# Sixteen blocks instead of thirteen fetched row by row by SyncE and ScalarE, in a gather and scatter kernel of a graph network

## The reference

```python
h = jnp.maximum(_layernorm(x, axis=-1), 0.0)
h0 = pe_val @ W0 + b0
t = gelu(h0) @ W1 + b1
t = gelu(t) @ W2 + b2
score = (h0 + t) @ W3 + b3
msg = h[src] * score
sums = segment_sum(msg, dst, num_segments=n)
cnt = segment_sum(ones, dst, num_segments=n)
out = x + (sums / jnp.maximum(cnt, 1.0)) @ Wo + bo
```

## Time and profile before

| | |
|---|---|
| median of 3 runs | 3926.53 us (3926.48 to 3933.37) |
| profiled execution, its time | 3928.06 us |
| profiled execution, its span | 3926.3 us |
| mean granted TensorE clock | 0.788 |
| PE busy | 3063.5 us, 78% |
| POOL busy | 2948.4 us, 75% |
| DVE busy | 1299.3 us, 33% |
| ACT busy | 850.0 us, 22% |
| row transfers on SPq | 7904 |
| row transfers on ACTq | 5408 |

### The profile page before, as it was taken

The page is one execution under the profiler, slowest core; times in us unless marked ns, Lnnn a source line. Parts: engine busy times, 40 slices in busy tenths (PEclk is TensorE's granted clock), DMA queues, the critical chain, the costliest instruction groups (busy, mean ns, idle before and its releaser), DMA issues.

```text
span 3926.3 us, 55941 instructions
## 1 busy us (share of the span) xinstructions
PE 3063.5 (78%) x8729; PEld 1466.1 (37%) x8730; DVE 1299.3 (33%) x2572; ACT 850.0 (22%) x1241; POOL 2948.4 (75%) x3125
## 2 busy tenths in 40 slices
PE   3886878777778778778877778788778777778778
PEld 1443333333333333333333333333333333333345
DVE  7333323333223333223333223333223333223334
ACT  4222212122222222222122212122222122222111
POOL 7777777777777777777777777777777777777775
PEclk9888778778777778778778777777777778778767
DMA  6122221111111111111111111111111111111112
GB/s 161 42 44 44 44 43 42 41 41 42 41 41 41 44 39 44 39 44 41 41 41 41 41 41 41 43 42 39 44 41 41 41 41 41 41 41 41 44 35 58
DMA packets 164649, 176.52 MB, mean 45 GB/s; under 512 B 86257, under 2 KB 86386, under 8 KB 163984
## 3 DMA queue, kind: packets, MB, share of 16 engines
q0 software_dynamic: 99808, 102.40, 13.7%
q1 hardware_dynamic: 53112, 67.00, 6.0%
q10 hardware_dynamic: 11432, 4.61, 0.4%
HBM read 167.34 MB, written 6.40 MB: 44 GB/s over the span
## 4 chain that ended last, share of the span: by engine, by line
POOL 61%; issue 21%; PE 11%; SPq 2%; DMA 2%; DVE 1%; ACTq 1%; ACT 0%; DVEq 0%; POOLq 0%
POOL rows L414 61%; DMA rows<-h_rows,idx 2%; SPq L367 2%; PE ps_wb L613 1%; PE ps_wa L613 1%; PE ps_h1a L593 1%; PE ps_h1a L590 1%; PE ps_h1b L583 1%; PE ps_h1b L593 1%; PE ps_sb L602 1%; ACTq L542 1%; PE ps_h1b L590 1%; PE ps_sa L602 1%; PE ps_h1a L583 1%; PE ps_h0b L574 1%
## 5 line engine op out<-in xcount | busy, mean ns | idle before, releaser
L414 POOL DMA_INDIRECT rows<-h_rows,idx x3071 | 2902.4, 945 | 937.0 <-issue 924.5
L613 PE MATMUL ps_wb<-ln_sq,msg 128*128 128x128 f32 x1608 | 324.0, 364 | 447.8 <-DVE acc L970 437.5
L844 DVE TENSOR_TENSOR msg<-ps_sb,rows 128x512 f32<-128x512 f32 x194 | 133.9, 690 | 1162.2 <-DMA rows<-h_rows,idx 1162.2
L844 DVE TENSOR_TENSOR msg<-ps_sa,rows 128x512 f32<-128x512 f32 x196 | 135.3, 691 | 1142.5 <-DMA rows<-h_rows,idx 1142.5
L613 PE MATMUL ps_wa<-ln_sq,msg 128*128 128x128 f32 x1616 | 289.5, 334 | 284.5 <-DVE acc L970 278.3
L613 PEld LDWEIGHTS ps_wb<-ln_sq,msg 128*128 128x128 f32 x1608 | 275.7, 259 | 611.3 <-DVE acc L970 563.7
L964 DVE TENSOR_REDUCE hot_sum<-ln_sq 128x64 f32<-128x512 f32 x403 | 415.1, 1030 | 13.3
L613 PEld LDWEIGHTS ps_wa<-ln_sq,msg 128*128 128x128 f32 x1616 | 245.1, 232 | 443.6 <-DVE acc L970 398.0
L486 ACT ACTIVATE score_t<-ps_h1a,b_last 128x512 f32<-128x512 f32 x202 | 138.9, 688 | 1094.5 <-PE ps_h1a L593 974.9
L486 ACT ACTIVATE score_t<-ps_h1b,b_last 128x512 f32<-128x512 f32 x201 | 138.2, 687 | 894.6 <-PE ps_h1b L593 767.8
L590 PE MATMUL ps_h1a<-attr,w_attr 64*128 64x512 f32 x404 | 319.3, 881 | 0.0
(11 more groups left out here) (102 smaller groups left out, 2096.4 us busy)
## 6 DMA issues: line engine op xcount, KB each, us to landing
ln_sq<-h_rows SPq DMA_DIRECT2D x7904, 0.2 KB
ln_sq<-h_rows ACTq DMA_DIRECT2D x5408, 0.2 KB
attr<-in_edges SPq DMA_DIRECT2D x201, 256.0 KB
rows<-h_rows,idx POOLq DMA_INDIRECT x3071, 2.6
xs<-in_x SPq DMA_DIRECT2D x4, 700.0 KB
h_rows<-ln_d ACTq DMA_DIRECT2D x4, 700.0 KB
dst_i<-in_dst SPq DMA_DIRECT2D x1, 1612.0 KB, 26.9
rows<-in_dst_rows SPq DMA_DIRECT2D x4, 384.0 KB
```

What stands on the lines that cost most here:

```text
L414: pool.indirect_dma_start(rows[:, slot, t, :], None, table, bass.IndirectOffsetOnAxis(ap=idx[:, s, t:t + 1], axis=0),).then_inc(gathered[s ...
L613: pe.matmul(window[0:m * D, 0:m * WIN], msg[:, s % 2, t:t + m, :].rearrange("p t d -> p (t d)"), hot[:, k, t:t + m, :].rearrange("p t n -> ...
L844: dve.tensor_tensor(msg[:, s % 2, 0:n, :], ps_s[s % 2][:, 0:n * D].rearrange("p (t d) -> p t d", d=D), near, ALU.mult).then_inc(msg_done, 1)
```

## The change

PERIOD goes from 31 to 25, so 16 blocks are fetched row by row: 23, 48, and so on to 398 (SPARE_AT = PERIOD - 2). SyncE brings 18 parts of each (576 rows) and ScalarE 14 (448 rows). SyncE's count of rows ahead of each attr load goes from 20 to 24 per block, ScalarE's from twice 7 to twice 9 per step. In all SyncE issues 9216 rows instead of 7904, ScalarE 7168 instead of 5408, and GpSimd 24 gathers fewer.

```diff
-PERIOD = 31
+PERIOD = 25
 SPARE_AT = PERIOD - 2
 SPARES = len(range(SPARE_AT, NB, PERIOD))
 SPARE_BUFS = 2
 LOADED = 32
...
-SP_PARTS = 19
-SP_ROWS = 20
-ACT_ROWS = 7
+SP_PARTS = 18
+SP_ROWS = 24
+ACT_ROWS = 9
```

## The result

| | before | changed |
|---|---|---|
| median | 3926.51 us (3925.52 to 3933.37, 4 runs) | 4022.89 us (4020.37 to 4029.74, 4 runs) |
| span of the profiled execution | 3926.3 us | 4020.3 us |
| mean granted TensorE clock | 0.788 | 0.791 |
| DVE line 844 waiting for gathered rows | 2304.7 us | not in the list |
| PE waiting for attr | 31.7 us | 788.2 us |

The changed kernel is 2.5% slower; 4013 us was forecast, with a range of 3978 to 4038 us.

The account below looks back on a forecast made before the run. SyncE's queue, with attr behind 24 rows per block (9.81 us), was to replace GpSimd as bound: last attr landed at 3843 us, plus 43, 57, 60 and 10 us of tail, gave 4013 us, range 3978 to 4038 us.

Parts of the forecast that it names:

- GpSimd's saving: On GpSimd's gather queue: three more blocks left out, 24 gathers at 1.250 us each, so the gathers end 30.0 us earlier.
- SyncE's pace: SyncE's queue: 24 row issues per block ahead of attr cost 9.81 us a block, against GpSimd's 9.6 us.
- the saturated stretch: Early part of SyncE's queue, attr issues from 163.0 to 544.4 us, giving 12.80 us per part of 32 rows.
- Fixed order, not the sum: SyncE's queue: attr stands behind (c - 5) x 24 rows for block c, so attr decides for the first 390 blocks.
- Rival A: GpSimd stays the bound because SyncE's 3841 us just fits on totals; 3897 us, chance 6%.
- Rival B: A saturated SyncE part costs only 12.50 us, so gain and cost cancel; 3926 us, unchanged, chance 3%.
- ScalarE's late rows: Last ScalarE rows of each row-fetched block come 2 or 3 steps later; the message stalls, SyncE does not; put at 0.
- rival C: Stalls at row-fetched blocks are not made good; some 14 blocks each add a 9.8 us step; 4150 us, chance 5%.
- That wait: TensorE waiting for attr: about 1200 us in all, 4 us a block over 300 blocks, where it was 31.7 us.
- The reserve of 4 us a block: Compute's slack, 9.81 - 5.8 us per block, taken as cover for the stalls at row-fetched blocks.
- The end: Tail after SyncE's last part at 3841 us: message(392), projection, nine messages at 60 us, then 10 us, ending at 4013 us.
- sign for a wrong end: In the profile after: the forecast of the tail is wrong if message(402) is not 160 us behind SyncE's last part.

## Why the prediction was right

- **GpSimd's saving, 30.0 us**: right. It showed as 29.9 us at message(392) once a quarter of SyncE's rows was left out, and as 29.5 us with 23 rows per block.
- **SyncE's pace, 9.81 us a block**: right, 9.80 measured; the last part at 3841 us was 3839. That pace makes 12.79 us for a part, so 12.80 from the saturated stretch was the better choice than 12.73 from the whole run. Why is open: ScalarE's rows make a part dearer (0.087 us), but they stood beside SyncE's parts before the change too. With 12.73 the forecast would have been 20 us lower and still inside the range.
- **Fixed order, not the sum, decides**: right, and the rows per block ahead of attr alone moved the time by -93 and +133 us. Rival A (the queue fits on totals, 3897 us) did not come true with 23 rows per block either: GpSimd's saving was there at message(392), but the last of the 288 parts came too late for message(398), and the kernel took 3930.03 us. With one part of each block moved to ScalarE as well it took 3896.46 us. The Trainium skill's rule that initiation is usually small relative to the DMA itself (DMA: Bandwidth & Descriptors, "Issuing engines are not separate DMA queues") did not carry over: the issue of 9216 rows of 256 bytes became the bound. Rival B needed a part of 12.50 us; even without ScalarE's rows a part took 12.7 us.
- **ScalarE's late rows hold up nobody on SyncE**: right. SyncE waited 1.3 us up to the last part, so rival C had no place. All of ScalarE's rows together are not free, though: left out, they made the span 55 us shorter, 25 us by cheaper parts on SyncE and 30 us in the tail, where the prediction had 8.2 us a step for them instead of 5.8.
- **That wait, 1200 us**: mis-sized, 788 us measured. The reserve of 4 us a block was given twice, once as cover for the stalls and once as a wait; that is an account and was not tested. Without ScalarE's rows, and with stalls of 60.0 us instead of 231.3, the wait was 1071.6 us; what the rest up to 1200 us is was not looked for. The time did not hang on this number.
- **The end, 172 us from the last part to the end of the span**: 181 measured (3839.1 to 4020.3). From the last part to message(392) 51 us instead of 45, then 53 instead of 57, then 67 instead of 60, of which some 10 us are the stall behind the output stores, for which the prediction had no term. These 9 us, less 2 us for the earlier last part, are the difference between 4013 and 4020.3 us of span. The prediction's own sign for a wrong end came: message(402) is 171 us behind the last part and not 160. With the stores moved it is 162 us. In part the terms of the end cancel: they were off by 6, -4 and 7 us.
- **GpSimd at the end**: the gathers of block 402 waited for the score of 393, until 3942.28 us; 3941 was forecast. The first row-fetched message came at 312.11 us; 311 was forecast.
- **Its sums**: five steps at 8.2 us are 41 us and not 43, 0.9 + 18 x 0.33 + 18/32 x 2.3 is 8.1 us and not 8.2, and the range goes up by 25 us where its upper bounds add up to 22. None of this decides.
- Messages of ordinary blocks were not evenly in pairs 19.6 us apart: the stalls at every twenty-fifth block bunch them.

## What to carry to other kernels

A queue that counts as idle in the profile can be the next bound. Work out its time per block in the order in which it is issued, with all that stands ahead of the item that the others wait for, and compare that with the bound's pace; 24 instead of 23 rows ahead of one load cost 93 us here. When work is moved off a saturated engine, each receiving queue must stay below the pace that is left, and must be done before a tail that nothing covers: with 23 rows the pace was low enough, and the late end of the same rows still cost all of the 30 us that had been saved.

## What the runs showed of the hardware

- ScalarE's row issues slow SyncE's: a part of 32 rows on SyncE took 0.087 us less with ScalarE's rows left out, 25 us over 288 parts (one run). Whether SyncE's rows slow ScalarE's was not tried.
- Two stores of 3 MB in all from SyncE's queue held ScalarE's queue up: nine row issues with a register load between them took 13.8 to 16.0 us in four kernels where others took 5.4 to 5.7. In the changed kernel the load took 8.2 us instead of 2.3. With the stores elsewhere, no such pause was left. By what way the one holds up the other was not tried.
